# A graph layer with a routed feed-forward: the last graph's feed-forward in two halves

## What is computed

```python
x = x + gnn(layernorm(x), adj, ...)          # convolution part; its result is x1 here
xf = layernorm(x1)                           # x2 in the kernel
logits = xf @ router_w + router_b
topw, topi = top_k(logits, 2); w = softmax(topw)
mask[node, topi] = w                         # 4 weights a node, two are zero
h = silu(einsum('td,edh->teh', xf, expert_w) + expert_b)
comb = einsum('te,teh->th', mask, h)
y = xf + comb @ out_w + out_b
out = x1 + norm_w * y / rms(y)
```

## Time and profile before

| What | Value |
|---|---|
| Median of 3 runs | 768.7 us (768.4 to 768.98) |
| The profiled execution | 771.66 us |
| Its span in the trace | 770.1 us |
| TensorE busy | 714.9 us, 93% |
| VectorE busy | 653.1 us, 85% |
| ScalarE busy | 468.3 us, 61% |
| GpSimd busy | 266.5 us, 35% |

### The profile page before, as it was taken

One profiled execution on the slowest core, in us unless ns is written; L12 is line 12 of the kernel. 1 busy time (PEld: TensorE's weight loads), 2 busy tenths in 40 slices (PEclk: granted clock), 3 DMA queues, 4 the chain that ended last, 5 costly groups with the idle time before them and its releaser, 6 DMA issues.

```text
span 770.1 us, 16492 instructions
## 1 busy us (share of the span) xinstructions
PE 714.9 (93%) x5593; PEld 488.5 (63%) x5593; DVE 653.1 (85%) x1544; ACT 468.3 (61%) x896; POOL 266.5 (35%) x638
## 2 busy tenths in 40 slices
PE   4788999999999999999999999999999999999772
PEld 3365584857768485766758585766848576675631
DVE  4878988899998889899888989999888989988662
ACT  4545757566585847657484756658584765746431
POOL 3132424152443515243352515244351514343201
PEclk9989999999999999999999999999999999999986
DMA  8427528284663828375471918456272827444131
GB/s 289 158 48 227 110 67 229 35 237 93 187 140 88 211 64 234 56 218 109 146 180 59 241 28 239 88 189 138 91 210 64 237 52 218 82 114 79 56 55 27
DMA packets 40712, 103.79 MB, mean 135 GB/s; under 512 B 4336, under 2 KB 5232, under 8 KB 40688
## 3 DMA queue, kind: packets, MB, share of 16 engines
q1 hardware_dynamic: 29168, 69.92, 27.7%
q0 software_dynamic: 11520, 33.56, 24.1%
HBM read 69.91 MB, written 16.78 MB: 113 GB/s over the span
## 4 chain that ended last, share of the span: by engine, by line
PE 63%; DVE 23%; issue 5%; DMA 3%; ACT 3%; POOL 1%; SPq 1%; DVEq 0%; POOLq 0%; ACTq 0%
PE bank L1051 16%; PE bank L1052 15%; PE bank L1053 15%; PE bank L1139 4%; PE bank L1138 4%; PE bank L1106 4%; DVE a1l L807 3%; DVE ybn L883 2%; DVE x L877 2%; DVE xtl L935 2%; DVE h L631 2%; DVE xbn L640 2%; DVE yf L866 2%; PE bank L1099 2%; DMA xb<-xn 1%
## 5 line engine op out<-in xcount | busy, mean ns | idle before, releaser
L456 ACT ACTIVATE silu<-bank,ebcol,ksc 128x512 f32<-128x512 f32 x128 | 98.8, 772 | 47.6 <-PE bank L1053 47.1
L1051 PE MATMUL bank<-xth,ewh 128*128 128x512 f16 x256 | 98.0, 383 | 1.4 <-DVE ewl L671 1.4
L1052 PE MATMUL bank<-xtl,ewh 128*128 128x512 f16 x256 | 97.9, 382 | 0.0
L1053 PE MATMUL bank<-xth,ewl 128*128 128x512 f16 x256 | 97.8, 382 | 0.0
L382 POOL TENSOR_TENSOR yme<-yms,epsrms 128x4 f32<-128x4 f32 (+1 forms) x17 | 3.3, 193 | 272.3 <-ACT ysq L491 272.3
L1051 PE MATMUL bank<-w2h,hnth 128*128 128x256 f16 x256 | 70.6, 276 | 0.0
L1052 PE MATMUL bank<-w2l,hnth 128*128 128x256 f16 x256 | 70.5, 276 | 0.0
L1053 PE MATMUL bank<-w2h,hntl 128*128 128x256 f16 x256 | 70.5, 275 | 0.0
L474 ACT ACTIVATE hnth<-bank 128x512 f16<-128x512 f32 x64 | 38.0, 594 | 39.1 <-PE bank L1106 39.1
L497 ACT ACTIVATE a1h<-bank,be 128x256 f16<-128x256 f32 x64 | 26.8, 470 | 56.0 <-PE bank L1190 52.7
L1189 PE MATMUL bank<-xsh,h 128*128 128x256 f16 x256 | 59.8, 281 | 0.8 <-DVE xsl L653 0.8
(11 more groups left out here) (207 smaller groups left out, 2070.3 us busy)
## 6 DMA issues: line engine op xcount, KB each, us to landing
adjin<-adj SPq DMA_DIRECT2D x16, 1024.0 KB, 5.4
adjtin<-adjt SPq DMA_DIRECT2D x16, 1024.0 KB, 6.3
xin<-x SPq DMA_DIRECT2D x16, 512.0 KB, 4.2
xb<-xn SPq DMA_DIRECT2D x16, 512.0 KB, 8.5
xb<-x POOLq DMA_DIRECT2D x16, 512.0 KB, 8.7
xb<-b POOLq DMA_DIRECT2D x16, 512.0 KB, 5.4
out<-x SPq DMA_DIRECT2D x16, 512.0 KB, 6.8
x2o<-ob SPq DMA_DIRECT2D x16, 512.0 KB, 10.5
```

The lines of the kernel that those rows point to most:

```text
L456: af(silu[:, i % 4, :], bank[E_BANK[i]][:, :], ACT.Silu, bias=ebcol[:, i:i + 1], scale=ksc[:, 2:3]).then_inc(silu_dn, 1)
L1051: mm(outp, lh, rh, start=first, stop=False)
L1052: mm(outp, lh, rl, start=False, stop=False)
L1053: return mm(outp, ll, rh, start=False, stop=last)
```

## The change

In `body(N - 1)` the `out_product`s, `y_part`s, squares and root of graph 14 are left out. `body(N)` and `body(N + 1)` are replaced by a `tail` on every engine.

- TensorE's tail starts with both `out_product`s of graph 14, so they run behind B3 of graph 15. VectorE's `y_part(14)` and ScalarE's squares follow, also the root and `finish(14)`.
- The feed-forward of graph 15 runs in halves h = 0, 1 of 256 nodes: transposes, router, `route`, mask, the four experts (each with both output halves, 256 columns a matmul), mask rows, weighing. The sums of half 0 over the experts are made by GpSimd, 128x512 each (`last_sum`); those of half 1 by VectorE (`last_add`). `last_ct(0)` on ScalarE waits for the three sums and stands ahead of the silu of experts 2 and 3 of half 1.
- `ob` is loaded into `xin` instead of `x2o`, well before, and x2 is added there. `y` is made a tile of 128 nodes at a time. VectorE multiplies y by norm_w while the root is made, then makes the finished output in one step (root times that, plus x1) in `xn`; SyncE stores it plainly: one DMA of 256 KB for half 0, two of 128 KB for half 1. x1 of graph 15 is not stored by itself.

```diff
             body(eng, N - 1, conv=True, ffn=True, late=True, prep=False)
-            body(eng, N, conv=False, ffn=True, late=True, prep=False)
-            body(eng, N + 1, conv=False, ffn=False, late=True, prep=False)
+            tail(eng)
...
+            def tail(sp):
+                sp.wait_ge(xn_dn, 4 * N)
+                sp.dma_start(xin[:, :, :], ob).then_inc(last_ob, 16)
+                sp.wait_ge(last_dn, CG)
+                sp.dma_start(out[LAST][:, 0:CG, :], xn[:, 0:CG, :]).then_inc(last_st, 16)
+                for t in range(CG, CT):
+                    sp.wait_ge(last_dn, t + 1)
+                    sp.dma_start(out[LAST][:, t:t + 1, :], xn[:, t:t + 1, :]).then_inc(last_st, 16)
...
+            def tail(gp):
+                gp.wait_ge(x2_dn, 4 * LAST + 4)
+                gp.wait_ge(last_ob, 16)
+                tt(spare_p[:, :], mone[:, 0:1], mone[:, 0:1], ALU.mult)
+                gp.dma_start(xin[:, :, :], x2[:, :, :], accum_op=ALU.add).then_inc(x2o_dn, 16)
+                roots_y(LAST - 1, ALL, 0)
+                s = slice(0, T_ROW)
+                for e in range(1, NE):
+                    gp.wait_ge(comb_st, 7 * LAST + e + 1)
+                    if e > 1:
+                        gp.wait_ge(last_sum, e - 1)
+                    tt(comb[:, :, s], comb[:, :, s], last_silu(e)[:, :, s], ALU.add).then_inc(last_sum, 1)
+                for j in range(2):
+                    add_yf(LAST - 1, j)
+                for j in range(2):
+                    roots_y(LAST, slice(CG * j, CG * j + CG), 2 * j)
...
+            def tail(act):
+                x2_part(act, LAST, 0)
+                last_xt(act, 0)
+                x2_part(act, LAST, 1)
+                squares(act, LAST - 1, 0)
+                squares(act, LAST - 1, 1)
+                last_tanh(act, 0)
+                last_xt(act, 1)
+                last_experts(act, 0, 0)
...
+                last_experts(act, 1, 1)
+                last_ct(act, 0)
+                last_experts(act, 1, 2)
+                last_experts(act, 1, 3)
+                last_ct(act, 1)
...
+            def tail(dve):
+                x1_half(LAST, 0, True)
+                stats_x1(LAST, 0)
+                x1_half(LAST, 1, True)
+                stats_x1(LAST, 1)
+                y_part(LAST - 1, 0)
+                y_part(LAST - 1, 1)
+                last_xt(0)
+                last_route(0)
+                last_xt(1)
+                last_mask(0)
+                last_route(1)
+                last_mask(1)
+                for e in range(NE):
+                    last_weigh(0, e)
+                finish(LAST - 1, (0, 1), False, True)
+                last_weigh(1, 0)
+                finish(LAST - 1, (2, 3), False, False)
+                last_weigh(1, 1)
+                last_add(1)
+                last_ct(0)
+                last_weigh(1, 2)
+                last_add(2)
+                last_weigh(1, 3)
+                last_add(3)
+                last_sum_y(0)
+                last_ct(1)
+                last_weigh_y(0)
+                last_out(0)
+                last_sum_y(1)
+                last_weigh_y(1)
+                last_out(1)
...
+            def tail(pe):
+                out_product(LAST - 1, 0)
+                out_product(LAST - 1, 1)
+                last_turn(0)
+                last_router(0)
+                last_experts(0, 0)
+                last_turn(1)
+                last_experts(0, 1)
+                last_router(1)
+                last_experts(0, 2)
+                last_turn_mask(0)
+                last_experts(0, 3)
+                last_rows(0)
+                last_turn_mask(1)
+                last_experts(1, 0)
+                last_rows(1)
+                last_experts(1, 1)
+                last_experts(1, 2)
+                last_experts(1, 3)
+                last_out(0)
+                last_out(1)
```

More of the change, by code:

```diff
@@ L210, in build, with last_silu, steps @@
         w_cur, x2o_set, x2o_dn = sem("w_cur"), sem("x2o_set"), sem("x2o_dn")
-        def steps(eng, body):
+        LAST = N - 1
+        def last_silu(e):
+            return (silu if e < 2 else r)[:, 2 * (e % 2):2 * (e % 2) + 2, :]
+        T_E, T_XT, T_R, T_MB, T_O, T_ROW = (1, 2, 5), (5, 0), (3, 4), ((6, 7), (0, 3)), (6, 7, 4, 5), CG * P
+        def steps(eng, body, tail):
             body(eng, 0, conv=True, ffn=False, late=False, prep=True)
@@ L358, in body @@
                     for j in range(2):
[L359 to L364, removed]
+                        add_yf(q, j)
                 if prep and ffn:
@@ L377, in body @@
                     add_b2(g)
[L378 to L384, removed]
+                if ffn and prep:
+                    roots_y(f, ALL, 0)
                 if conv:
@@ L605, in body, with last_experts @@
                     setup_hi(c_scale, ((rwf, rwh, RW), (owf, owh, OW)), c_hi)
-                if ffn:
+                if ffn and prep:
                     squares(act, f, 0)
                     squares(act, f, 1)
-            steps(act, body)
+            def last_experts(act, h, e):
+                c = slice(T_ROW * h, T_ROW * h + T_ROW)
+                act.wait_ge(e_rdy, 8 * LAST + 4 * h + e + 1)
+                for m in range(2):
+                    i = 2 * e + m
+                    b = bank[T_E[(4 * h + e) % 3]][:, T_ROW * m:T_ROW * m + T_ROW]
+                    af(last_silu(e)[:, m, c], b, ACT.Silu, bias=ebcol[:, i:i + 1], scale=ksc[:, 2:3]).then_inc(silu_dn, 1)
@@ L612, in _ @@
+            steps(act, body, tail)
         @block.vector
@@ new lines, in last_add, with last_ct, last_sum_y @@
+            def last_add(e):
+                c = slice(T_ROW, 2 * T_ROW)
+                dve.wait_ge(comb_st, 7 * LAST + 4 + 2 * e)
+                TT(comb[:, :, c], comb[:, :, c], last_silu(e)[:, :, c], ALU.add).then_inc(comb_st, 1)
+            def last_ct(h):
+                c = slice(T_ROW * h, T_ROW * h + T_ROW)
+                dve.wait_ge(ct_hi, 2 * LAST + h + 1)
+                STT(ctl[:, :, c], comb[:, :, c], ksc[:, 5:6], cth[:, :, c], ALU.mult, ALU.subtract).then_inc(ct_lo, 1)
+            def last_sum_y(h):
+                s = slice(CG * h, CG * h + CG)
+                dve.wait_ge(o_rdy, 2 * LAST + h + 1)
+                if h == 0:
+                    dve.wait_ge(x2o_dn, 16 * LAST + 16)
+                for t in range(CG * h, CG * h + CG):
+                    STT(y[:, t, :], bank[T_O[t]][:, 0:D], ksc[:, 3:4], xin[:, t, :], ALU.mult, ALU.add).then_inc(last_y, 1)
@@ new lines, in last_weigh_y, with last_out @@
+            def last_weigh_y(h):
+                s = slice(CG * h, CG * h + CG)
+                dve.wait_ge(last_y, CG * h + CG)
+                TT(xb[:, s, :], y[:, s, :], nwb[:, :].unsqueeze(1).to_broadcast([P, CG, D]), ALU.mult).then_inc(last_w, 1)
+            def last_out(h):
+                dve.wait_ge(last_w, h + 1)
+                dve.wait_ge(rr_st, 2 * LAST + 2 * h + 2)
+                for t in range(CG * h, CG * h + CG):
+                    STT(xn[:, t, :], xb[:, t, :], yrr[:, t:t + 1], x1[:, t, :], ALU.mult, ALU.add).then_inc(last_dn, 1)
@@ L1045, in _ @@
+            steps(dve, body, tail)
         @block.tensor
@@ new lines, in last_experts @@
+            def last_experts(h, e):
+                u = 4 * h + e
+                c = slice(T_ROW * h, T_ROW * h + T_ROW)
+                if u < 3:
+                    pe.wait_ge(x1_dn, 4 * N)
+                else:
+                    pe.wait_ge(silu_dn, 8 * LAST + 2 * (u - 3) + 2)
+                for m in range(2):
+                    i = 2 * e + m
+                    b = bank[T_E[u % 3]][:, T_ROW * m:T_ROW * m + T_ROW]
+                    for k in range(KD):
+                        ins = three(b, ewh[:, k, P * i:P * i + P], ewl[:, k, P * i:P * i + P], xth[:, k, c], xtl[:, k, c],
+                                    k == 0, k == KD - 1)
+                ins.then_inc(e_rdy, 1)
@@ new lines, in last_out, with part @@
+            def last_out(h):
+                def part(first):
+                    for t in range(CG):
+                        b = bank[T_O[CG * h + t]][:, 0:D]
+                        c = slice(T_ROW * h + P * t, T_ROW * h + P * t + P)
+                        for k in range(KD):
+                            if first:
+                                mm(b, cth[:, k, c], owh[:, k, :], start=(k == 0), stop=False)
+                                mm(b, cth[:, k, c], owl[:, k, :], start=False, stop=False)
+                            else:
+                                ins = mm(b, ctl[:, k, c], owh[:, k, :], start=False, stop=(k == KD - 1))
+                    if not first:
+                        ins.then_inc(o_rdy, 1)
+                pe.wait_ge(ct_hi, 2 * LAST + h + 1)
+                part(True)
+                pe.wait_ge(ct_lo, 2 * LAST + h + 1)
+                part(False)
```

138 lines of the change are left out of this document (127 added, 11 removed).

## The result

| | before | changed |
|---|---|---|
| Median | 768.55 us (4 runs, 767.46 to 768.98) | 759.28 us (4 runs, 757.32 to 761.25) |
| Ratio | | 0.9873, 95% interval 0.9854 to 0.9893 |
| Profiled execution | 771.66 us | 757.32 us |
| Its span | 770.1 us | 755.8 us |

What follows compares the result with a forecast made beforehand. TensorE was taken as the bound for the middle graphs, untouched; only the tail changes. Gains 0.78 + 2.74 - 0.81 + 2.66 + 5.23 = 10.6 us give span 759.5, time 758.1 us; own range 756.8 to 759.4, wider 755.4 to 762.5.

Steps and rivals of the forecast that it cites:

- A: Last `v_tile`'s end to x1 of graph 15: moving graph 14's out products gains 0.78 us, 8.60 to 7.82.
- D: Last sum's end to the last store's issue: 7.37 us, a gain of 2.66.
- B: x1 of graph 15 to the first weighing: 13.86 us instead of 16.60, a gain of 2.74 through halves.
- C: First weighing to the last sum's end: 11.30 us instead of 10.49, a loss of 0.81, GpSimd's sums stretched by collision.
- E: Last store's issue to the span's end: 3.3 us instead of 8.53, a gain of 5.23 from the plain store.
- the signs that the prediction had named for its own failure: Long GpSimd drain, sums far from 1.3 to 2 us, or VectorE, not GpSimd, stretched where they meet.
- Rival 5: Stage to x1: moving the out products gains and hides nothing, 0.78 us back, 758.9 us; chance 0.50 shared with the forecast.
- Rival 2: Before the first weighing: granted clock falls to 1.2 GHz, 0.9 to 2.6 us lost, 759.0 to 760.7; chance 0.18.
- Rivals 3 and 4: GpSimd's sums: short without collision, 756.3 us, chance 0.13; or gating everything, 770.7 us at 6 us each, chance 0.04.
- I take it as over: Kernel's end: GpSimd's drain assumed finished, its last DMAs going out nine us ahead of its end at 755.2.
- Rival 1: Kernel's end: GpSimd's drain stays, 8.3 us after the last root whatever lies ahead, 762.3 us; chance 0.15.
- carry-over: Whole kernel: the profiled execution's 3.0 us above the median persists, turning a span of 759.5 into 758.1 us.

Runs made afterwards that it cites:

- the move alone: Kernel before, with only graph 14's out products, y, squares and root placed behind graph 15's last incidence product; 766.13 us, ratio 0.9956.
- filled before: Kernel before, with 86 extra unread matmuls in TensorE's gaps of the last feed-forward; 764.94 us, ratio 0.994.
- the reordered variant: Changed kernel with y of half 1 first, 34 filling matmuls, both `finish` behind the first weighing and the out-product copies moved back; 759.51 us, ratio 0.9867.
- the repeated run: Changed kernel measured once more with no edit; 758.36 us, ratio 0.9844 to the kernel before.
- the best that computes the reference: Changed kernel with y of half 1 ahead of half 0's output on VectorE, plus 34 filling matmuls; 757.25 us, ratio 0.9838, tail 42.13 us.
- the accumulating variant: Changed kernel, but graph 15's x1 stored by SyncE and yf added by GpSimd's accumulating DMAs, as before; 763.07 us, ratio 0.9919.

## Why the prediction came out right, step by step

The time was right; A and D were right for the reasons given, and in B, C and E luck had a part. Two of the signs that the prediction had named for its own failure appeared: the drain is long, and VectorE, not GpSimd, is stretched where they meet.

**A was right in size and reason.** A forecast gain of 0.78, 0.77 measured, 0.76 in the move alone and given back in full when the move is undone. Rival 5 (the move gives nothing) is out.

**B was right in one execution and hides a second one.** 13.86 was forecast at full clock and the first profile shows 13.77. But six profiles have this stage unaltered and without fillers: the clock held in two (13.77, 13.76) and fell in four, with 15.07 to 15.33. Rival 2's mechanism is no rare case: it came 6.3 to 6.9 us behind the start of x1, around TensorE's 1.41 us wait for `xtl`, where the prediction had 8.3; its price of 0.9 to 2.6 was right at 1.3 to 1.6, and its chance of 0.18 was far too small. The median of 759.28 lies in rival 2's range, that of 758.36 beside the forecast; both are inside the forecast's own range.

The gain in B is also less the halves' doing than the prediction's working suggests. It compared a new stage at full clock with an old one at 0.50. Between kernels whose clock holds in both (filled before, changed) B gains 14.59 - 13.77 = 0.82 and not 2.74. The whole tail gains 50.66 - 43.33 = 7.3 there; the other 3.6 of the 10.92 is clock that the kernel before loses and this execution of the new one does not.

**C was near in size by luck, by a wrong mechanism.** The step that failed is "`finish(14)` has two such inputs, so I add its 1.65" to GpSimd's sums. GpSimd's three sums took 1.27 us each, the forecast size, and were over at 739.53. VectorE's four `finish` instructions took 1.5 us more than without the sums, and VectorE, never idle from 734.07 to 744.83, set C's length. The row that misled me was GpSimd's tiny multiplication held for 1.18 us; but there VectorE's instruction had begun 0.10 us earlier. In the long overlaps of these traces the instruction that began second was held by the first: `finish` behind the sums, and in the reordered variant GpSimd's third sum behind VectorE's. The wrong step left the sum near the mark only because 1.5 us on the one engine replaced 1.65 on the other. The rule of the Trainium skill (GPSIMD Engine Reference, Key points) holds as to the contention, and as to VectorE being about twice as fast at elementwise work (0.69 us against 1.27 for a sum). Even so the sums on VectorE cost 0.72 us more here, where the prediction called it about the same. Rivals 3 and 4 are out: no sum was short, none was near 5 us.

**D: the sum held, 7.57 for 7.37.** The idle waits for the roots are 0.94 and 1.17 us. The remark that `last_out(0)` blocks `last_sum_y(1)` for about 1 us is shown, with a condition that it lacked: 1.1 to 1.2 us come back if TensorE's clock is up when the second out product runs, 0.3 if it is not.

**E: the size by luck, two errors that cancel.** "I take it as over" is wrong. The drain ends 4.1 us behind GpSimd's last root, in all nine profiles that keep these roots and the plain store, so it ends the kernel, 0.9 us late. Against that the store landed in 2.0 us and not 2.4, and SyncE's way out took 0.4, not 0.9. Without the roots on GpSimd E is 2.4. Rival 1 was right that the drain stays and wrong on its length: 8.3 us is what follows a DMA issue, not a root. By the figures of the Trainium skill (DMA: Bandwidth & Descriptors, Anatomy of one DMA), which are for another kind of queue, 2.3 us is the estimate for the 128 KB; the trace has 2.0.

**Sum and carry-over.** 10.6 was forecast for the tail and 10.92 came, while the medians moved by 9.3 us (11.7 beside the repeated run). With the clock fallen in B, as in the repeated run's profile, the tail gives 54.25 - 44.71 = 9.5. That the profiled execution stood 3.0 above the median was carried over as a constant; it was of the size of the 3.38 us that lie between the two traces ahead of any changed line. The lower clock at 40 to 90 us stands beside them; no run shows that it is all of them.

**Open.** What decides whether the clock falls in B in a given execution was not found; TensorE's idle gaps ahead of the fall are 0.70 and 1.41 us whether it falls or not. The medians of the changed kernel and of its variants overlap within their intervals, so the order of the best ones rests on their traces: the best that computes the reference is 1.2 us shorter in its tail than the changed kernel with the clock up.

## What to carry to other kernels

In a kernel's last stage, cost each step at both levels of the granted clock: here one and the same stage differed by 1.4 us between executions, more than many an edit is worth. A few matmuls that nobody reads, put into real idle time and never in front of a product that is ready, test this cheaply. When two traces are compared, first subtract what they differ by ahead of the edit. An engine's drain at the end belongs on the list of what can end last, counted from that engine's last instruction, even where its transfers are long done. Where two engines collide, ask which instruction begins first.

## What the hardware did that I had not expected

- GpSimd's drain at the end lasts until 4.1 us after its last computing instruction where that comes last (nine profiles). Where an accumulating DMA comes last it lasts until 6.8 to 7.4 us after the end of its issue, which is 3.3 us after that DMA's landing (before, the move alone, the accumulating variant, before with fillers; 3.2 without the roots). At the kernel's start one lasted 0.18 us.
- Where GpSimd's 128x512 additions meet VectorE's instructions with two SBUF inputs, the one that began second was held by the other: VectorE's 0.87 us pairs took 1.93 and 1.28 beside sums of 1.27, and one sum of GpSimd took 1.53.
- The clock of one and the same program fell in the tail in some executions and not in others, for 1.4 us of time in B.
